# Attention probabilities kept whole in fp32, multiplied by the latent in two column groups

## The chip, the cores and the metric

The program runs on one core of one Trainium2 chip. The metric is the device time of one launch in microseconds, from the first to the last instruction of the core. Three runs of the kernel before gave 3666.07, 3667.09 and 3668.12 us, so the median is 3667.09 us. Times in the rows below are microseconds unless marked ns.

## The reference

One decoder layer over x of 4 x 512 x 1024 (fp32), in three parts, each followed by x + part and a layer norm:

- a gated state-space mixer (untouched by the change),
- cross attention against a context of 4 x 1601 x 1024, in which the change lies,
- a feed-forward network with int4-style weights (untouched).

The cross attention works through a latent of 64:

```python
C_q  = Q @ Wq_d                       # 512 x 128 per batch
C_kv = K @ Wkv_d                      # 1601 x 64 per batch: the latent
CqWqk = (C_q @ W_qk).reshape(b, n, H, LKV)              # 16 heads of 64
scores = einsum('bnhl,bkl->bhnk', CqWqk, C_kv) / sqrt(64)
attn = softmax(scores, axis=-1)
V_up = (C_kv @ Wv_u).reshape(b, nkv, H, HD)
out  = einsum('bhnk,bkhd->bnhd', attn, V_up)
```

The kernel uses that attn @ (C_kv @ Wv) = (attn @ C_kv) @ Wv: the probabilities are first multiplied by the latent (1601 x 64), the small result then by the head's 64 x 64 of Wv.

## The kernel before, in words

The three parts run one after the other, with a barrier of all engines between them. `attention` holds its order by hand: each engine has its own program, and semaphores tie them. There are 4 batches of 16 heads (g counts 64 heads), and a head has 4 units q of 128 queries. Units 0 and 1 are pair s=0, units 2 and 3 are pair s=1.

Ahead of the heads of a batch, the latent is computed on TensorE (L653, plain fp32), ScalarE rounds it to fp32r (`kh`), and VectorE subtracts to get the rest (`kl`, also fp32r). Both halves are turned by TensorE (L677, stationary 64 x 128, 64 columns streamed) and VectorE copies them to `cn`, 13 tiles of 128 keys x 128, where columns 0 to 63 are the high half and 64 to 127 the low half. The queries' projection is L667 (plain fp32, 512 columns) and, once per head, L589.

One unit goes through these steps:

- scores: 4 column chunks of the PSUM tile `sc`, each as two fp32r products with `kh` and `kl` (L696);
- `mx`, `nm` on VectorE (L860, L862, L866), then exp on ScalarE in two halves (L784), 1024 and 577 keys;
- the next unit's scores may overwrite a half of `sc` as soon as that half's exp is done;
- turns: 13 transposes of 128 x 128 (L618) into three PSUM tiles `tp`, in groups of 4, 4, 4 and 1, with group 3 of both units of a pair taken together. `TURNS` lists the 14 turns of a head. Each turn is emptied first by ScalarE, which writes the fp32r half `pth` (L742 and L739), then by VectorE, which subtracts to get `ptl` (L821 and L817);
- `weigh(g, s, part)`: `po` gathers cn.T @ pth and cn.T @ ptl for a pair, 26 fp32r products of 256 columns (two units of 128 queries), 13 in part 0 and 13 in part 1 (L629). The two 64-row halves of `po` hold the products with the latent's high and low half.

Once per head, ScalarE copies `po` to `ot` (L749), and `output` multiplies `ot` by Wv, stacked twice over 128 rows so that the two halves are added (4 products of 64 columns, L642). VectorE scales by the softmax sum (L836) and GpSimd adds to `y` (L921).

TensorE's order inside a unit is: scores of unit q, transposes of unit q-1, one weigh part, then a leftover: at q=0 the last turn of the head before, at q=1 the next head's projection, at q=2 turn 6, at q=3 the output of the head before. VectorE's order is: two maxima, `nm`, the three subtractions of unit q-1, then the same leftovers. ScalarE's is: three casts of unit q-1, the two exps of unit q, the leftovers.

The edits touch `tensor`, `scalar` and `vector` inside `attention`, the semaphores and the tiles above them.

Of the kernel before, what the change touches and what calls it, by code (L numbers as in the profile page):

```python
# [4 lines left out]
F32 = mybir.dt.float32  # L5
F32R = mybir.dt.float32r
I32 = mybir.dt.int32
ALU = mybir.AluOpType
# [3 lines left out]
P = 128  # L12
# [489 lines left out]
TURNS = [g for s in (0, 2) for g in (*((s + z, 1, k) for z in (0, 1) for k in range(3)), (s, 2, 3))]  # L502
NTURN = len(TURNS)
UNITS = QT
NHEAD = L * HEADS


def attention(nc, d, x1, x2):

    with ExitStack() as ctx:  # L510
# [9 lines left out]
        s_zero, s_y0 = sem("zero"), sem("y0")  # L520
        s_kv, s_kh, s_kl = sem("kv"), sem("kh"), sem("kl")
# [3 lines left out]
        s_tr, s_ph, s_pl, s_pv, s_ot = (sem(n) for n in ("tr", "ph", "pl", "pv", "ot"))  # L525
        s_sm, s_rd, s_op, s_yo, s_ya = (sem(n) for n in ("sm", "rd", "out_ps", "yo", "ya"))
        s_own, s_var, s_std, s_norm = sem("vector_own"), sem("var"), sem("std"), sem("norm")
# [54 lines left out]
        def tensor():  # L582
            T.wait_ge(small, 32)

            def project(g):
                T.wait_ge(s_wq, g + 1)
                if g % HEADS:
                    T.wait_ge(s_pl, (g - 1) * NTURN + 1)
                T.matmul(tp[0][:, :], wqs[:, g % 2, :, :].rearrange("p a e -> p (a e)"), cq[:, :],  # L589
                         start=True, stop=True).then_inc(s_q, 1)  # L590

            def turn(g, e):
                u, units, k, ng, s = turn_of(g, e)
                T.wait_ge(s_ex, (g * UNITS + u + units) * 2)
                if k in (1, 2):
                    if u or g % HEADS:
                        T.wait_ge(s_pl, g * NTURN + e - (3 if e in (1, 2, 8, 9) else 2))
                elif k == 3:
                    T.wait_ge(s_pl, g * NTURN + e - 2)
                elif u == 1 or u == 3:  # L600
                    if u == 1 and g % HEADS < HEADS - 1:
                        T.wait_ge(s_ql, g + 2)
                    elif u == 1:
                        T.wait_ge(s_pl, g * NTURN + 1)
                    elif u == 3 and g % HEADS:
                        T.wait_ge(s_yo, g)
                    else:
                        T.wait_ge(s_pl, g * NTURN + 8)
                elif u == 2:
                    T.wait_ge(s_pl, g * NTURN + 7)  # L610
                elif g % HEADS:
                    T.wait_ge(s_pl, g * NTURN)
                else:
                    T.wait_ge(s_ql, g + 1)
                n = 0
                for z in range(units):
                    for c in range(4 * k, 4 * k + ng):
                        ins = T.transpose(tp[k % 3][:, n * P:(n + 1) * P], pr[u + z][:, c * P:(c + 1) * P], ident[:, :])  # L618
                        n += 1
                ins.then_inc(s_tr, 1)  # L620

            def weigh(g, s, part):
                if part == 0:
                    if g:
                        T.wait_ge(s_ot, g)
                    T.wait_ge(s_pl, g * NTURN + 7 * (s + 1))
                for n in range(part * NKT, (part + 1) * NKT):
                    t, src = n // 2, (pth, ptl)[n % 2]
                    ins = T.matmul(po[:, s * 256:(s + 1) * 256], cn[:, t, :], src[s][:, t, :],  # L629
                                   start=(n == 0), stop=(n == 2 * NKT - 1))  # L630
                if part == 1:
                    ins.then_inc(s_pv, 1)

            def output(g):
                T.wait_ge(s_ot, g + 1)
                if g % HEADS < HEADS - 1:
                    T.wait_ge(s_pl, (g + 1) * NTURN + 8)
                else:
                    T.wait_ge(s_pl, (g + 1) * NTURN)
                h = g % HEADS  # L640
                for q in range(QT):
                    ins = T.matmul(tp[0][:, q * LAT:(q + 1) * LAT], ot[:, q * P:(q + 1) * P],  # L642
                                   wv[:, h * LAT:(h + 1) * LAT], start=True, stop=True)
                ins.then_inc(s_op, 1)

            for b in range(L):
# [22 lines left out]
                for k in range(len(GROUPS)):  # L669
                    T.wait_ge(s_kl, b * NKC + k + 1)  # L670
# [10 lines left out]
                T.wait_ge(s_cn, (b + 1) * 4)  # L681

                g0 = b * HEADS
# [41 lines left out]
        def scalar():  # L725
# [7 lines left out]
            def turn(g, e):  # L733
                u, units, k, ng, s = turn_of(g, e)
                S.wait_ge(s_tr, g * NTURN + e + 1)
                if e % 7 == 0 and g:
                    S.wait_ge(s_pv, 2 * (g - 1) + s + 1)
                if units == 2:
                    S.copy(pth[s][:, 4 * k, 0:2 * P], tp[k % 3][:, 0:2 * P]).then_inc(s_ph, 1)  # L739
                else:  # L740
                    lo = (u % 2) * P
                    S.copy(pth[s][:, 4 * k:4 * k + ng, lo:lo + P],  # L742
                           tp[k % 3][:, 0:ng * P].rearrange("p (t e) -> p t e", e=P)).then_inc(s_ph, 1)

            def output(g):
                S.wait_ge(s_pv, 2 * (g + 1))
                if g:
                    S.wait_ge(s_op, g)
                S.copy(ot[:, :], po[:, :]).then_inc(s_ot, 1)  # L749
# [52 lines left out]
        def vector():  # L802
            own = 0
            for t in (kh, kl, *pr):
                ins = V.memset(t[:, NKV:KPAD].bitcast(F32) if t.dtype == F32R else t[:, NKV:KPAD], 0.0)
# [7 lines left out]
            def turn(g, e):  # L813
                u, units, k, ng, s = turn_of(g, e)
                V.wait_ge(s_ph, g * NTURN + e + 1)
                if units == 2:
                    V.tensor_tensor(ptl[s][:, 4 * k, 0:2 * P], tp[k % 3][:, 0:2 * P], pth[s][:, 4 * k, 0:2 * P].bitcast(F32),  # L817
                                    ALU.subtract).then_inc(s_pl, 1)
                else:
                    lo = (u % 2) * P  # L820
# [18 lines left out]
            for b in range(L):  # L839
# [7 lines left out]
                for k in range(len(GROUPS)):  # L847
                    V.wait_ge(s_cnp, b * 4 + k + 1)
                    V.tensor_copy(cn[:, 4 * k:4 * k + GROUPS[k], :],
                                  tp[k % 2][:, 0:GROUPS[k] * P].rearrange("p (t e) -> p t e", e=P)).then_inc(s_cn, 1)  # L850
                g0 = b * HEADS
# [535 lines left out]
```

## Time and profile before

| | us |
|---|---|
| median of 3 runs | 3667.09 |
| the profiled execution | 3671.16 |
| its span | 3669.4 |
| PE busy in the span | 3116.9 (85%) |
| DVE busy | 2895.4 (79%) |
| ACT busy | 1899.6 (52%) |
| POOL busy | 1484.0 (40%) |

The profiled execution took 4.07 us more than the median, 1.8 us of which lie outside its span. PE is TensorE's matmul side and PEld its weight loads, which can lie under matmuls. A busy PE is not PE at its peak: a record's duration holds latency as well, so the pace of a stream is read from the starts of its records and not from their mean duration. A plain fp32 product leaves two load records and two matmul records (L667: 32 products, 64 records of each), an fp32r product and a transpose leave one of each. The mixer lies at 0 to 396 us, attention at 396 to 2001 us and the feed-forward network behind it.

### The profile page before, as it was taken

What the parts mean: (1) busy time and instruction counts of PE and PEld (TensorE: products, weight loads), DVE (VectorE), ACT (ScalarE), POOL (GpSimd) and SP (SyncE); (2) the same over time, 40 slices, a digit from 0 to 9 for tenths busy, and PEclk for the clock granted to TensorE, in tenths of its full rate; (3) what the DMA queues carried; (4) which work ended last, traced back from release to release, by engine and by line L of the source; (5) the groups of instructions that cost most, each with busy time, mean ns of one, the idle gap of its engine ahead of it and who ended that gap; (6) DMA issues with size and microseconds to landing.
All of it is one profiled execution on the core that took longest, in us unless ns stands there. A gap on an engine that the chain in (4) does not pass through costs nothing. (4 is left out here: it accounts for less than half of the span.)

```text
span 3669.4 us, 45273 instructions
## 1 busy us (share of the span) xinstructions
PE 3116.9 (85%) x16232; PEld 2464.0 (67%) x16232; DVE 2895.4 (79%) x3593; ACT 1899.6 (52%) x3089; POOL 1484.0 (40%) x672
## 2 busy tenths in 40 slices
PE   6455599998999899989997788888986799888986
PEld 3332388867888588858886566666664566666665
DVE  1657288866887588848886799999997799999997
ACT  2223177745776377727775444454453444444443
POOL 0242000000000000000000588888884588888884
PEclk8777799999999899989998899999998899999998
DMA  4003600011000300010001423333232433323332
GB/s 144 0 0 125 222 1 1 1 66 53 1 1 1 118 1 1 1 49 1 1 1 49 152 103 121 120 107 134 104 120 86 157 109 110 131 104 128 113 110 85
DMA packets 86158, 269.25 MB, mean 73 GB/s; under 512 B 12209, under 2 KB 13234, under 8 KB 85938
## 3 DMA queue, kind: packets, MB, share of 16 engines
q1 hardware_dynamic: 81090, 248.02, 19.2%
q10 hardware_dynamic: 4848, 18.35, 1.2%
q8 instruction: 132, 2.16, 0.2%
q14 instruction: 88, 0.72, 0.1%
HBM read 241.17 MB, written 25.17 MB: 73 GB/s over the span
## 5 line engine op out<-in xcount | busy, mean ns | idle before, releaser
L1292 POOL TENSOR_TENSOR c_sum_u<-c_sum_u,c_scaled 128x1024 f32<-128x1024 f32 x276 | 744.1, 2696 | 76.4 <-ACT c_scaled L1132 63.1
L1132 ACT ACTIVATE c_scaled<-c_ps,c_scol 128x1024 f32<-128x1024 f32 x448 | 498.1, 1118 | 501.2 <-PE c_ps L1081 305.3
L1201 DVE SCALAR_TENSOR_TENSOR c_acc<-c_ps,c_sd,c_acc 128x1024 f32<-128x1024 f32 x448 | 555.5, 1275 | 65.5 <-PE c_ps L1081 65.3
L742 ACT CAST b_pth<-b_tp 128x512 fp32r<-128x512 f32 x768 | 401.8, 596 | 376.4 <-PE b_tp L618 376.4
L921 POOL TENSOR_TENSOR b_y<-b_y,b_yo 128x256 f32<-128x256 f32 x64 | 47.3, 739 | 1347.2 <-DVE b_yo L836 1347.2
L821 DVE TENSOR_TENSOR b_ptl<-b_tp,b_pth 128x512 fp32r<-128x512 f32 x768 | 480.9, 682 | 7.7 <-ACT b_pth L742 7.6
L784 ACT ACTIVATE b_pr<-b_sc,b_nm 128x1024 f32<-128x1024 f32 (+1 forms) x512 | 474.9, 941 | 0.9 <-DVE b_nm L866 0.6
L618 PE MATMUL b_tp<-b_ident,b_pr 128*128 128x128 f32 x3328 | 441.4, 277 | 12.1 <-DVE b_ptl L821 8.1
L1292 POOL TENSOR_TENSOR c_sum_g<-c_sum_g,c_scaled 128x1024 f32<-128x1024 f32 x164 | 427.3, 2605 | 34.0 <-ACT c_scaled L1132 27.6
L696 PE MATMUL b_sc<-b_kh,b_qs 128*128 128x512 f32 (+1 forms) x1024 | 395.8, 387 | 44.0 <-ACT b_pr L784 31.2
L629 PE MATMUL b_po<-b_ptl,b_cn 128*128 128x256 f32 x1664 | 418.8, 289 | 0.0
L629 PE MATMUL b_po<-b_pth,b_cn 128*128 128x256 f32 x1664 | 418.7, 289 | 0.0
L1081 PE MATMUL c_ps<-c_xh,c_gw_int 128*128 128x512 f32 x896 | 305.3, 423 | 108.6 <-DVE c_sum_g L1214 94.7
L618 PEld LDWEIGHTS b_tp<-b_ident,b_pr 128*128 128x128 f32 x3328 | 363.3, 141 | 19.5 <-issue 11.6
L860 DVE TENSOR_REDUCE b_mx<-b_sc 128x1 f32<-128x1024 f32 x256 | 312.2, 1220 | 73.1 <-PE b_sc L696 71.2
L1081 PE MATMUL c_ps<-c_xh,c_uw_int 128*128 128x512 f32 x896 | 291.7, 407 | 73.2 <-DVE c_acc L1201 44.3
L696 PE MATMUL b_sc<-b_kl,b_qs 128*128 128x512 f32 (+1 forms) x1024 | 345.6, 370 | 0.0
L1081 PE MATMUL c_ps<-c_hh,c_dw_int 128*128 128x512 f32 x896 | 297.1, 414 | 31.3 <-POOL c_hl L1299 27.4
L629 PEld LDWEIGHTS b_po<-b_ptl,b_cn 128*128 128x128 f32 x1664 | 317.3, 191 | 0.0
L629 PEld LDWEIGHTS b_po<-b_pth,b_cn 128*128 128x128 f32 x1664 | 317.2, 191 | 0.0
L1214 DVE SCALAR_TENSOR_TENSOR c_sum_g<-c_ps,c_scol,c_sum_g 128x1024 f32<-128x1024 f32 x224 | 286.2, 1278 | 17.5 <-ACT c_sum_g L1125 6.8
L1081 PEld LDWEIGHTS c_ps<-c_xh,c_gw_int 128*128 128x128 f32 x896 | 159.0, 193 | 201.4 <-DVE c_sum_g L1214 118.6
(184 smaller groups left out, 5345.5 us busy)
## 6 DMA issues: line engine op xcount, KB each, us to landing
c_gw<-in_c_gw SPq DMA_DIRECT2D x56, 512.0 KB, 6.6
c_gz<-in_c_gz SPq DMA_DIRECT2D x56, 512.0 KB, 7.4
c_uw<-in_c_uw SPq DMA_DIRECT2D x56, 512.0 KB, 8.2
c_uz<-in_c_uz SPq DMA_DIRECT2D x56, 512.0 KB, 9.0
c_dw<-in_c_dw SPq DMA_DIRECT2D x56, 512.0 KB, 3.2
c_dz<-in_c_dz SPq DMA_DIRECT2D x56, 512.0 KB, 5.7
b_cx<-in_b_ctxT SPq DMA_DIRECT2D x12, 2048.0 KB, 11.6
a_xt<-in_a_xT SPq DMA_DIRECT2D x4, 2048.0 KB, 11.8
```

Of the source, the lines that this page charges most:

```text
L618: ins = T.transpose(tp[k % 3][:, n * P:(n + 1) * P], pr[u + z][:, c * P:(c + 1) * P], ident[:, :])
L629: ins = T.matmul(po[:, s * 256:(s + 1) * 256], cn[:, t, :], src[s][:, t, :], start=(n == 0), stop=(n == 2 * NKT - 1))
L696: ins = T.matmul(sc[:, n * 512:n * 512 + w], qs[g % 2][:, q * P:(q + 1) * P], k[:, n * 512:n * 512 + w], start=(z == 0), stop=(z == 1))
L742: S.copy(pth[s][:, 4 * k:4 * k + ng, lo:lo + P], tp[k % 3][:, 0:ng * P].rearrange("p (t e) -> p t e", e=P)).then_inc(s_ph, 1)
L784: S.activation(pr[q][:, lo:hi], sc[:, lo:hi], ACT.Exp, bias=nm[:, q % 2:q % 2 + 1], scale=0.125, accum_out=den[:, g % 2, q, half:half + 1] ...
L821: V.tensor_tensor(ptl[s][:, 4 * k:4 * k + ng, lo:lo + P], tp[k % 3][:, 0:ng * P].rearrange("p (t e) -> p t e", e=P), pth[s][:, 4 * k:4 * k ...
L860: V.tensor_reduce(mx[:, 0:1], sc[:, 0:1024], AX, ALU.max).then_inc(s_ma, 1)
L1081: ins = T.matmul(pair[PLACE[x]][:, b * 512:(b + 1) * 512], w[n][t % 2][:, k * P:(k + 1) * P], v[:, b * 512:(b + 1) * 512], start=(z == 0), ...
L1132: S.activation(scaled[q % 2][:, :], ps[:, :], ACT.Identity, scale=column).then_inc(s_c, 1)
L1201: V.scalar_tensor_tensor(out=acc[:, k, :], in0=ps[:, :], scalar=sd[:, k, j - 1:j], in1=acc[:, k, :], op0=ALU.mult, op1=ALU.add).then_inc(s ...
L1214: V.scalar_tensor_tensor(out=total, in0=ps[:, :], scalar=column, in1=total, op0=ALU.mult, op1=ALU.add).then_inc(s_a[n], 1)
L1292: G.tensor_tensor(total, total, scaled[POOLED.index(x) % 2][:, :], ALU.add).then_inc(s_a[n], 1)
```

## The change

The turned probabilities are no longer split. Each turn is emptied once, as fp32, into `pt`: groups 0 and 3 by ScalarE (`BY_ACT`, 6 turns of a head), groups 1 and 2 by VectorE (`BY_DVE`, 8 turns). The latent is kept whole too: ScalarE copies the 64 rows of each chunk to `kf` ahead of `kh`, and `cn` has 64 columns per tile of keys. `weigh` gives each unit of a pair its own 64 columns of the array and its own 64 partitions of `po`: for each of the 13 tiles of keys two plain fp32 products of 128 columns, with the stationary `cn[:, t, :]` of 64 columns. `output` now contracts over 64 rows, units 0 and 2 first, then, after a wait for those, units 1 and 3. Where TensorE waited for `ptl`, it now waits for the one copy (`copied`). Scores, exp, projections and the other two parts of the layer are the same.

```diff
+BY_ACT = [e for e in range(NTURN) if TURNS[e][2] in (0, 3)]
+BY_DVE = [e for e in range(NTURN) if TURNS[e][2] in (1, 2)]
...
-        cn = sb("b_cn", [P, NKT, P], F32R)
+        cn = sb("b_cn", [P, NKT, LAT])
-        pth = [sb(f"b_pth{j}", [P, NKT, 2 * P], F32R) for j in range(2)]
-        ptl = [sb(f"b_ptl{j}", [P, NKT, 2 * P], F32R) for j in range(2)]
-        ot = sb("b_ot", [P, NB])
+        pt = [sb(f"b_pt{j}", [P, NKT, 2 * P]) for j in range(2)]
+        kf = sb("b_kf", [LAT, KPAD])
+        ot = sb("b_ot", [P, 2 * P])
...
+        def copied(eng, g, e):
+            if e in BY_ACT:
+                eng.wait_ge(s_pa, g * len(BY_ACT) + BY_ACT.index(e) + 1)
+            else:
+                eng.wait_ge(s_pd, g * len(BY_DVE) + BY_DVE.index(e) + 1)
...
 def weigh(g, s, part):
-                    T.wait_ge(s_pl, g * NTURN + 7 * (s + 1))
+                    copied(T, g, 7 * s + 6)
+                    copied(T, g, 7 * s + 5)
                 for n in range(part * NKT, (part + 1) * NKT):
-                    t, src = n // 2, (pth, ptl)[n % 2]
-                    ins = T.matmul(po[:, s * 256:(s + 1) * 256], cn[:, t, :], src[s][:, t, :],
-                                   start=(n == 0), stop=(n == 2 * NKT - 1))
+                    t, z = n // 2, n % 2
+                    ins = T.matmul(po[z * LAT:(z + 1) * LAT, s * P:(s + 1) * P], cn[:, t, :], pt[s][:, t, z * P:(z + 1) * P],
+                                   start=(t == 0), stop=(t == NKT - 1))
...
 def output(g):
-                for q in range(QT):
-                    ins = T.matmul(tp[0][:, q * LAT:(q + 1) * LAT], ot[:, q * P:(q + 1) * P],
-                                   wv[:, h * LAT:(h + 1) * LAT], start=True, stop=True)
-                ins.then_inc(s_op, 1)
+                for z in range(2):
+                    if z:
+                        T.wait_ge(s_oe, g + 1)
+                    for s in range(2):
+                        q = 2 * s + z
+                        ins = T.matmul(tp[0][:, q * LAT:(q + 1) * LAT], ot[z * LAT:(z + 1) * LAT, s * P:(s + 1) * P],
+                                       wv[z * LAT:(z + 1) * LAT, h * LAT:(h + 1) * LAT], start=True, stop=True)
+                    ins.then_inc(s_op if z else s_oe, 1)
...
 latent, per tile of keys (tensor)
-                        for z, src in enumerate((kh, kl)):
-                            ins = T.transpose(tp[k % 2][:, (t - 4 * k) * P + z * LAT:(t - 4 * k) * P + (z + 1) * LAT],
-                                              src[0:LAT, t * P:(t + 1) * P].bitcast(F32), ident[0:LAT, 0:LAT])
+                        ins = T.transpose(tp[k % 2][:, (t - 4 * k) * LAT:(t - 4 * k + 1) * LAT],
+                                          kf[:, t * P:(t + 1) * P], ident[0:LAT, 0:LAT])
...
 scalar
-                    S.copy(pth[s][:, 4 * k:4 * k + ng, lo:lo + P],
-                           tp[k % 3][:, 0:ng * P].rearrange("p (t e) -> p t e", e=P)).then_inc(s_ph, 1)
+                    S.copy(pt[s][:, 4 * k:4 * k + ng, lo:lo + P],
+                           tp[k % 3][:, 0:ng * P].rearrange("p (t e) -> p t e", e=P)).then_inc(s_pa, 1)
+                    S.copy(kf[:, n * 512:n * 512 + KCHUNK[n]], sc[0:LAT, n * 512:n * 512 + KCHUNK[n]]).then_inc(s_kf, 1)
...
 vector
-                    V.tensor_tensor(ptl[s][:, 4 * k:4 * k + ng, lo:lo + P],
-                                    tp[k % 3][:, 0:ng * P].rearrange("p (t e) -> p t e", e=P),
-                                    pth[s][:, 4 * k:4 * k + ng, lo:lo + P].bitcast(F32), ALU.subtract).then_inc(s_pl, 1)
+                V.tensor_copy(pt[s][:, 4 * k:4 * k + ng, lo:lo + P],
+                              tp[k % 3][:, 0:ng * P].rearrange("p (t e) -> p t e", e=P)).then_inc(s_pd, 1)
```

## Rows read from the trace of the kernel before

**Rows 1.** Busy time by stretch: mixer, heads of batch 0, feed-forward network
```profile
core 0: us, PE busy (x) PEld busy (x) DVE busy (x) ACT busy (x) POOL busy (x), PEclk, DMA share, GB/s
0.00:396.00 396.00, 207.06 (x705) 120.40 (x705) 194.31 (x345) 111.32 (x253) 89.47 (x36) 0.75 0.24 82
...
440.00:785.00 345.00, 330.93 (x2290) 294.47 (x2290) 280.45 (x475) 244.25 (x511) 14.44 (x29) 0.99 0.00 1
...
2001.00:3669.00 1668.00, 1403.11 (x5632) 1059.79 (x5632) 1510.63 (x1211) 781.33 (x740) 1317.33 (x504) 0.94 0.33 118
```
**Rows 2.** Waits, 396 to 2001 us: total us, times, longest
```profile
PE b_sc L696 <- ACT b_pr L784: 31.2, 75, 3.8
```
**Rows 3.** Timeline, unit q=2 of a head: start, us, engine, line
```profile
1406.41 0.50 PE L696 MATMUL b_sc<-b_kh,b_qs 128*128 128x512 f32 x1 [0.17 <-ACT b_pr L784]
...
1407.72 1.22 DVE L860 TENSOR_REDUCE b_mx<-b_sc 128x1 f32<-128x1024 f32 x1
...
1408.74 1.57 ACT L742 CAST b_pth<-b_tp 128x512 fp32r<-128x512 f32 x3 [0.91 <-PE b_tp L618]
1408.85 0.75 DVE L862 TENSOR_REDUCE b_mx<-b_sc 128x1 f32<-128x577 f32 x1
1409.71 0.21 DVE L866 TENSOR_SCALAR b_nm<-b_mx 128x1 f32<-128x1 f32 x1
...
1410.18 1.14 ACT L784 ACTIVATE b_pr<-b_sc,b_nm 128x1024 f32<-128x1024 f32 x1
...
1411.78 0.47 PE L696 MATMUL b_sc<-b_kh,b_qs 128*128 128x512 f32 x1
```
**Rows 4.** Groups of instructions by form: count | busy us, mean ns | idle
```profile
L821 DVE TENSOR_TENSOR b_ptl<-b_tp,b_pth 128x512 fp32r<-128x512 f32 x768 | 480.9, 682 | 7.7 <-ACT b_pth L742 7.6
L742 ACT CAST b_pth<-b_tp 128x512 fp32r<-128x512 f32 x768 | 401.8, 596 | 376.4 <-PE b_tp L618 376.4
L846 DVE COPY b_xT<-b_tp 128x512 f32<-128x512 f32 x16 | 11.1, 692 | 10.6 <-PE b_tp L661 10.6
```
**Rows 5.** Timeline, TensorE: last transposes, a weigh part, the output, the next scores
```profile
506.31 0.71 PE L618 MATMUL b_tp<-b_ident,b_pr 128*128 128x128 f32 x5
506.78 0.37 PE L629 MATMUL b_po<-b_pth,b_cn 128*128 128x256 f32 x1
506.98 0.28 PE L629 MATMUL b_po<-b_ptl,b_cn 128*128 128x256 f32 x1
...
508.30 0.28 PE L629 MATMUL b_po<-b_pth,b_cn 128*128 128x256 f32 x1
508.42 1.00 PE L642 MATMUL b_tp<-b_wv,b_ot 128*128 128x64 f32 x8
509.23 0.47 PE L696 MATMUL b_sc<-b_kh,b_qs 128*128 128x512 f32 x1
```
**Rows 6.** Timeline, TensorE: plain fp32 of 512 columns, then the latent's turns
```profile
429.31 7.11 PE L667 MATMUL b_po<-b_xT,b_wqd 128*128 128x512 f32 x16 [0.88 <-DVE b_xT L846]
436.34 0.27 PE L677 MATMUL b_tp<-b_ident,b_kh 64*128 64x64 f32 x1
436.46 0.22 PE L677 MATMUL b_tp<-b_ident,b_kl 64*128 64x64 f32 x1
...
436.95 0.22 PE L677 MATMUL b_tp<-b_ident,b_kl 64*128 64x64 f32 x1
```
**Rows 7.** Timeline: products of 4 columns, whose loads set the pace
```profile
113.69 1.40 PE L155 MATMUL a_ps<-a_fcd,a_xst 128*128 128x4 f32 x12
```
**Rows 8.** Timeline: VectorE behind an output, and a load under a matmul
```profile
508.18 0.28 PE L629 MATMUL b_po<-b_ptl,b_cn 128*128 128x256 f32 x1
508.18 0.19 PEld L629 LDWEIGHTS b_po<-b_pth,b_cn 128*128 128x128 f32 x1
...
509.46 0.42 DVE L836 TENSOR_TENSOR b_yo<-b_tp,b_rd 128x256 f32<-128x256 f32 x1 [0.29 <-PE b_tp L642]
509.96 0.74 POOL L921 TENSOR_TENSOR b_y<-b_y,b_yo 128x256 f32<-128x256 f32 x1 [20.04 <-DVE b_yo L836]
```

More of the change, by code:

```diff
@@ L520, in attention @@
         s_zero, s_y0 = sem("zero"), sem("y0")
-        s_kv, s_kh, s_kl = sem("kv"), sem("kh"), sem("kl")
+        s_kv, s_kh, s_kf, s_kl = sem("kv"), sem("kh"), sem("kf"), sem("kl")
         s_xt, s_xa, s_xd, s_cqp, s_cq, s_cnp, s_cn = (sem(n) for n in ("xt", "xt_act", "xt_dve", "cq_ps", "cq", "cn_ps", "cn"))
@@ L524, in attention @@
         s_sa, s_sb, s_ma, s_mb, s_nm, s_ex = (sem(n) for n in ("sa", "sb", "max_a", "max_b", "nm", "ex"))
-        s_tr, s_ph, s_pl, s_pv, s_ot = (sem(n) for n in ("tr", "ph", "pl", "pv", "ot"))
-        s_sm, s_rd, s_op, s_yo, s_ya = (sem(n) for n in ("sm", "rd", "out_ps", "yo", "ya"))
+        s_tr, s_pa, s_pd, s_pv, s_ot = (sem(n) for n in ("tr", "p_act", "p_dve", "pv", "ot"))
+        s_sm, s_rd, s_oe, s_op, s_yo, s_ya = (sem(n) for n in ("sm", "rd", "out_even", "out_ps", "yo", "ya"))
         s_own, s_var, s_std, s_norm = sem("vector_own"), sem("var"), sem("std"), sem("norm")
@@ L587, in project @@
                 if g % HEADS:
-                    T.wait_ge(s_pl, (g - 1) * NTURN + 1)
+                    copied(T, g - 1, 0)
                 T.matmul(tp[0][:, :], wqs[:, g % 2, :, :].rearrange("p a e -> p (a e)"), cq[:, :],
@@ L595, in turn @@
                 if k in (1, 2):
-                    if u or g % HEADS:
-                        T.wait_ge(s_pl, g * NTURN + e - (3 if e in (1, 2, 8, 9) else 2))
+                    if u:
+                        copied(T, g, e - (4 if u == 2 else 3))
+                    elif g % HEADS:
+                        copied(T, g - 1, e + 10)
                 elif k == 3:
-                    T.wait_ge(s_pl, g * NTURN + e - 2)
+                    copied(T, g, e - 3)
                 elif u == 1 or u == 3:
@@ L603, in turn @@
                     elif u == 1:
-                        T.wait_ge(s_pl, g * NTURN + 1)
+                        copied(T, g, 0)
                     elif u == 3 and g % HEADS:
@@ L607, in turn @@
                     else:
-                        T.wait_ge(s_pl, g * NTURN + 8)
+                        copied(T, g, 7)
                 elif u == 2:
-                    T.wait_ge(s_pl, g * NTURN + 7)
+                    copied(T, g, 6)
                 elif g % HEADS:
-                    T.wait_ge(s_pl, g * NTURN)
+                    copied(T, g - 1, 13)
                 else:
@@ L636, in output @@
                 if g % HEADS < HEADS - 1:
[L637 removed]
+                    copied(T, g + 1, 7)
                 else:
[L639 removed]
+                    copied(T, g, 13)
                 h = g % HEADS
[L641 to L644 removed]
+                for z in range(2):
[6 more added lines that the diff above has]
+                    ins.then_inc(s_op if z else s_oe, 1)
             for b in range(L):
@@ L669, in tensor @@
                 for k in range(len(GROUPS)):
-                    T.wait_ge(s_kl, b * NKC + k + 1)
+                    T.wait_ge(s_kf, b * NKC + k + 1)
                     if k == 0:
@@ L681, in tensor @@
                 T.wait_ge(s_cn, (b + 1) * 4)
+                T.wait_ge(s_kl, (b + 1) * NKC)
                 g0 = b * HEADS
@@ L734, in turn @@
                 u, units, k, ng, s = turn_of(g, e)
+                if e not in BY_ACT:
+                    return
                 S.wait_ge(s_tr, g * NTURN + e + 1)
@@ L738, in turn @@
                 if units == 2:
-                    S.copy(pth[s][:, 4 * k, 0:2 * P], tp[k % 3][:, 0:2 * P]).then_inc(s_ph, 1)
+                    S.copy(pt[s][:, 4 * k, 0:2 * P], tp[k % 3][:, 0:2 * P]).then_inc(s_pa, 1)
                 else:
                     lo = (u % 2) * P
-                    S.copy(pth[s][:, 4 * k:4 * k + ng, lo:lo + P],
-                           tp[k % 3][:, 0:ng * P].rearrange("p (t e) -> p t e", e=P)).then_inc(s_ph, 1)
+                    S.copy(pt[s][:, 4 * k:4 * k + ng, lo:lo + P],
+                           tp[k % 3][:, 0:ng * P].rearrange("p (t e) -> p t e", e=P)).then_inc(s_pa, 1)
             def output(g):
@@ L748, in output @@
                     S.wait_ge(s_op, g)
-                S.copy(ot[:, :], po[:, :]).then_inc(s_ot, 1)
+                S.copy(ot[:, :], po[:, 0:2 * P]).then_inc(s_ot, 1)
             for b in range(L):
@@ L803, in vector @@
             own = 0
-            for t in (kh, kl, *pr):
+            for t in (kh, kl, kf, *pr):
                 ins = V.memset(t[:, NKV:KPAD].bitcast(F32) if t.dtype == F32R else t[:, NKV:KPAD], 0.0)
@@ L814, in turn @@
                 u, units, k, ng, s = turn_of(g, e)
[L815 to L820, printed above, removed]
-                    V.tensor_tensor(ptl[s][:, 4 * k:4 * k + ng, lo:lo + P],
-                                    tp[k % 3][:, 0:ng * P].rearrange("p (t e) -> p t e", e=P),
-                                    pth[s][:, 4 * k:4 * k + ng, lo:lo + P].bitcast(F32), ALU.subtract).then_inc(s_pl, 1)
+                if e not in BY_DVE:
+                    return
+                V.wait_ge(s_tr, g * NTURN + e + 1)
+                if e % 7 == 1 and g:
+                    V.wait_ge(s_pv, 2 * (g - 1) + s + 1)
+                lo = (u % 2) * P
+                V.tensor_copy(pt[s][:, 4 * k:4 * k + ng, lo:lo + P],
+                              tp[k % 3][:, 0:ng * P].rearrange("p (t e) -> p t e", e=P)).then_inc(s_pd, 1)
             def sums(g):
@@ L849, in vector @@
                     V.tensor_copy(cn[:, 4 * k:4 * k + GROUPS[k], :],
-                                  tp[k % 2][:, 0:GROUPS[k] * P].rearrange("p (t e) -> p t e", e=P)).then_inc(s_cn, 1)
+                                  tp[k % 2][:, 0:GROUPS[k] * LAT].rearrange("p (t e) -> p t e", e=LAT)).then_inc(s_cn, 1)
                 g0 = b * HEADS
```

## The prediction

> **What bounds the kernel now.** I read the stretches first: the mixer and the feed-forward network keep their work, so their 396 and 1668 us stay, and the change is worth what it is worth among the heads. There TensorE is busy 330.93 of 345 us, with the granted clock at 0.99, the level of 2.4 GHz [rows 1]. The waits say the same: over all of attention TensorE's scores wait 31.2 us for the exp that frees `sc`, and no other engine holds it up for more [rows 2]. A head takes 0.74 + 20.04 = 20.78 us by GpSimd's add, which comes once per head [rows 8]. That is 5.2 us per unit.
>
> A second loop is nearly as long, though. Read unit q=2 in order of time [rows 3]: the scores start at 1406.41, the first maximum at 1407.72, the second at 1408.85, `nm` ends at 1409.92, but the exp starts at 1410.18, because ScalarE has been in its three casts since 1408.74. The exp ends at 1411.32 and the next scores start at 1411.78, when TensorE is through with the output. So this loop could turn in about 4.9 us against TensorE's 5.2. Two conclusions: added TensorE time goes into the end almost in full, and saved TensorE time pays until the unit nears 4.9 us. What VectorE and ScalarE save pays almost nothing by itself.
>
> **The weigh parts (256 of them, 64 heads by 4).** One takes 508.42 - 506.78 = 1.64 us: 13 records at (508.30 - 506.98)/11 = 0.120 us each are 1.56, and 0.08 lies at the entry [rows 5]. After the change a part has 13 plain fp32 products, so 26 records of 128 columns. The streaming rate of plain fp32 is in the 16 records of 512 columns: (436.34 - 429.31)/16 = 0.439 us, or 0.110 us for 128 columns [rows 6]. The load need not add to it: a load starts with the matmul ahead of it, at 508.18 both [rows 8], and loads of 128 columns, bare of streaming, follow each other every 1.40/12 = 0.117 us at most [rows 7]; these have 64 columns.
>
> Everything hangs on whether the products of the two units, in two column groups, run beside each other. No row shows a product in a column group, so the price is bounded from both sides. One after the other: 26 x 0.110 = 2.86 us. Side by side, with unit 1's first record under unit 0's second and so on: half, 0.055 us per record, 1.43 us. Nothing below that, since each group alone must stream 13 x 0.110. A floor near it is in the trace: load and matmul pairs of the latent's turns follow each other every (436.95 - 436.46)/8 = 0.061 us [rows 6], so the queue can hand out pairs at about the rate wanted. I take side by side, at 0.058 us between these two: 26 x 0.058 = 1.51 against 1.56, or -0.05 x 256 = -13 us. I take it because the two groups share neither stationary, nor moving data, nor output partitions, and only order in one queue ties them.
>
> The Trainium skill, "TensorE: Matmul & The Clock Gate", Part 3, says that matmuls on different tiles of the array run concurrently and reports 2.38 times for three column tiles of 32. No run here shows it so far; by it alone a part would cost some 1.4 to 1.8 us.
>
> **Changing between whole-array and column-group work.** Each part is now preceded and followed by products of the whole array, 8 changes per head, 512 in all. The nearest row: entering the 64-row turns, the first record takes 0.12 us instead of 0.061, so 0.06 [rows 6], where the entry of a weigh part costs 0.08 already [rows 5]. That makes the extra 0. The other end is a whole latency of a record: 0.22 long at a pace of 0.061, so 0.16 us [rows 6], 82 us in all. I take 0.04, nearer to the row: +20 us.
>
> **The output (64 times).** Eight records take 509.23 - 508.42 = 0.81 us, 0.101 each, and the last one ends 1.00 - 7 x 0.101 = 0.29 after it starts [rows 5]. Now four records, then a wait for their end, then four. VectorE starts 0.04 us after that last end (509.42 to 509.46) [rows 8]; with the same delay the second four start at 3 x 0.101 + 0.29 + 0.04 = 0.63, pay an entry of 0.08, and end at 0.63 + 0.08 + 0.40 = 1.11. That is +0.30, or +20 us; bounds +13 (no entry) to +40 (two changes of the array at 0.16 on top). Behind the waiting product in TensorE's queue are the next head's scores of unit 0, and behind these the maxima, so this is on the path.
>
> **Relief.** VectorE has 8 copies instead of 12 + 2 subtractions in a head, at 0.69 (the copy of a PSUM tile) against 0.68 us; ScalarE loses 8 casts of 0.6 us, 4.8 us per head [rows 4]. TensorE is never fed by them for long, so it counts where TensorE stands: the 0.26 us by which casts hold the exp in unit q=2 [rows 3] comes off waits of 31.2 us in all [rows 2], into which part of the added time falls too. Bounds -25 and 0; I take -8.
>
> **Once per batch.** 52 of the 104 turns of the latent go, at 0.061 [rows 6]: -3 us. The `kf` copies lie under the next chunk's products except the last, short one: +1. Behind the last unit the subtraction that followed the cast goes: -2. Together -4 us.
>
> **Sum.** -13 + 20 + 20 - 8 - 4 = +15 us on the profiled execution's 3671.2, so 3686; this execution is 4 us over the median, so 3682. A change under 0.2% (7.3 us) can't be told from none.
>
> **Rivals.**
> - *One after the other.* The second unit's products don't start before the first's have streamed. Then a part takes 26 x 0.110 + 0.08 = 2.94 us, +1.30 x 256 = +333; with +20 for the output, -4, and about -10 for waits that this fills, +340: 4007 us. For it: no row shows two products streaming at once, and the records of one engine run in order. At the pace of the bare loads, 0.117 [rows 7], it would be 4054.
> - *Faster: pairs at the full rate.* Its place is the weigh part, its price the pace of a record. At 0.055 the parts give -0.13 x 256 = -33; with no cost for changes, +20 for the output, -20 for relief and -4: -37, so 3630 us. With the terms at my values for output, changes, relief and batches (+28), it turns into a gain under (1.56 - 28/256)/26 = 0.0558 us per record; without the cost of changes, already under 0.0596. Against it: the only pace shown for such short pairs is 0.061.
> - *The changes cost a full emptying.* 0.16 for each of 512 and of 128 more around the outputs: +102 in place of +20; with -13, +20 and -4 that is +105: 3772 us. What speaks for it is that a record's 0.16 of latency exists; against it, that entering the 64-row turns cost 0.06.
>
> The Trainium skill states this last one as a rule: "TensorEngine Tiling (Array Packing)", Key Properties, says that changing the tiling mode drains TensorE. The 0.06 of the row doesn't bear out a full emptying, and by the rule the sum would be the rival's.
>
> - *Half beside each other*, because loads or the two records of a product hold each other up: between, about 3850 us.
>
> **How the numbers follow.** Side by side as forecast 0.33 (own range 3645 to 3740), one after the other 0.30, full rate 0.20, full emptying 0.12, half 0.05. The likeliest gives 3682. The range takes in most of the full-rate case and the one-after-the-other case up to 4020: 3635 to 4020. Faster by over 0.2%: the full-rate case and a low end of the forecast's, 0.26. Within 0.2%: 0.09. Slower: 0.65, of which nearly half is the serial case.
>
> **What would show it.** In the timeline of TensorE, 26 records of a part in about 1.5 us, with starts two to a step of 0.11; a serial case shows 2.9 us, a head of 26 us, and no waits for the exp. Parts that enter or leave with gaps over 0.1 us show the emptying. The output should span 1.1 us. VectorE's busy time should fall by about 3.4 us per head and ScalarE's by 4.8 without TensorE's waits vanishing. The stretches of mixer and feed-forward network should be unmoved; if they move, or the granted clock among the heads leaves 0.98, the prediction is wrong for a reason that it doesn't hold.

## The result and the profile after

The changed kernel takes 3695.86 us (median of 4 runs, 3692.24 to 3700.31) against 3667.61 us for the kernel before beside it (4 runs): ratio 1.0078, 95% interval 1.0061 to 1.0096. It is 28 us slower, where +15 was forecast (3682 us). The profiled execution took 3693.81 us with a span of 3692.0.

The page first, then the stretches [rows 1]: the heads of batch 0 still fill 440 to 785 us, and the other stretch is within the feed-forward network.

```profile
span 3692.0 us, 51078 instructions
PE 3162.8 (86%) x19508; PEld 2445.4 (66%) x19508; DVE 2698.0 (73%) x3210; ACT 1661.3 (45%) x2593; POOL 1485.6 (40%) x672
...
L640 PE MATMUL b_po<-b_pt,b_cn 128*64 128x128 f32 x6656 | 443.5, 276 | 0.0
```

```profile
440.00:785.00 345.00, 340.71 (x3065) 289.24 (x3066) 228.47 (x375) 180.99 (x381) 14.10 (x28) 0.99 0.01 1
2001.00:3669.00 1668.00, 1401.40 (x5766) 1059.71 (x5764) 1515.57 (x1194) 777.68 (x741) 1320.58 (x506) 0.94 0.32 115
```

VectorE's and ScalarE's busy time have fallen by 52 and 63 us in the first stretch, TensorE's has risen by 10, and the granted clock is 0.99 as before. TensorE is now busy 340.71 of 345 us, so it still bounds the heads. Now the timeline of TensorE around one part and the output, which answers to [rows 5]:

```profile
1403.73 1.53 PE L628 MATMUL b_tp<-b_ident,b_pr 128*128 128x128 f32 x12
1405.19 1.74 PE L640 MATMUL b_po<-b_pt,b_cn 128*64 128x128 f32 x26
1406.86 1.37 PE L657 MATMUL b_tp<-b_wv,b_ot 64*128 64x64 f32 x8
1408.16 0.50 PE L711 MATMUL b_sc<-b_kh,b_qs 128*128 128x512 f32 x1
```

Three things are to be seen. First, the 26 records of the part start 0.059 us apart on average, (1.74 - 0.272)/25, so the two units do run side by side. The average hides how. Here are the first two and the last two records of this part, each pair from a window of its own:

```profile
1405.19 0.33 PE L640 MATMUL b_po<-b_pt,b_cn 128*64 128x128 f32 x2
1406.55 0.38 PE L640 MATMUL b_po<-b_pt,b_cn 128*64 128x128 f32 x2
```

A record is 0.32 us long at the entry and 0.27 at the end of a part, so the first two start 0.007 us apart and the last two 0.109. The trace's start times say the same of all 244 parts whose records stand in it whole: 12 pairs, one of each column group, 0.160 us from the first pair to the second and 0.109 from then on, and at the end two single records. A part has 13 products, 7 of one unit and 6 of the other. The last product has no partner, so a part takes 14 steps of 0.109 us and not 13.

Second, the 12 transposes, which took 1.28 us to the next start before, take 1405.19 - 1403.73 = 1.46. Third, the output takes 1.30 us instead of 0.81.

The waits, 396 to 2030 us, over which the four batches now stretch. The first row is of the kernel before (396 to 2001 us), the other two of the changed one:

```profile
PEld b_sc L696 <- ACT b_pr L784: 89.7, 192, 4.0
```
```profile
PEld b_sc L711 <- ACT b_pr L802: 27.8, 17, 4.0
PE b_sc L711 <- ACT b_pr L802: 23.1, 11, 3.9
```

The matmul row fell by 8 us only [rows 2], but the row of the loads fell by 62 and from 192 times to 17, where attention has 256 units. The start times show what is meant. They need one correction of the rows ahead of the prediction: the unit that [rows 3] shows, and that the prediction reads, is q=3 and not q=2, for the output stands behind it. In the kernel before, the two transposes ahead of its scores took 0.55 us to the next start, in the changed one they take 0.34, and 0.20 ahead of the scores of q=1:

```profile
1405.86 0.38 PE L618 MATMUL b_tp<-b_ident,b_pr 128*128 128x128 f32 x2
...
1406.41 0.50 PE L696 MATMUL b_sc<-b_kh,b_qs 128*128 128x512 f32 x1 [0.17 <-ACT b_pr L784]
```
```profile
1401.75 0.44 PE L628 MATMUL b_tp<-b_ident,b_pr 128*128 128x128 f32 x2
1402.09 0.50 PE L711 MATMUL b_sc<-b_kh,b_qs 128*128 128x512 f32 x1
...
1412.91 0.44 PE L628 MATMUL b_tp<-b_ident,b_pr 128*128 128x128 f32 x2
1413.11 0.48 PE L711 MATMUL b_sc<-b_kh,b_qs 128*128 128x512 f32 x1
```

By start-to-start times over all heads, what moved is this. The two middle columns are medians, worked out from the two traces; the last one is the difference of the sums, since some kinds of stretch come in two lengths.

| stretch of TensorE, to the next start | before | after | times | us |
|---|---|---|---|---|
| 12 transposes, then a part | 1.284 | 1.459 | 244 | +43 |
| a weigh part, then another stretch | 1.638 | 1.673 | 236 | +8 |
| output | 0.812 | 1.298 | 56 | +27 |
| 2 transposes, then scores | 0.495 | 0.195 | 120 | -31 |
| the next head's projection, then scores | 0.588 | 0.562 | 64 | -5 |
| a weigh part, then scores at once | 2.223 | 1.794 | 8 | -3 |
| scores of a unit | 1.632 | 1.633 | 248 | +3 |

That is +42; the stretches of the heads, from first to last `nm` of a batch, grew by 41 us in all. From the last latent product to the first `nm` each batch is 1.1 to 2.3 us shorter, -6 us in all. The spans differ by only 22.6 us. The rest, -13 us, lies in the mixer, the feed-forward network and the starts of batches. The edit doesn't touch the mixer, and yet it ends (by the start of the first latent product) at 396.0 us before and 390.5 after; over all kernels here its end lies between 389.6 and 398.2 us. So a difference of a few us between two kernels is to be looked for in the heads before it is believed.

### The profile page after: what moved, and what is told of

The parts are those of the page before. It is cut to its first block and busy times, and to the rows that moved or that the text cites. A ratio compares the mean times of both kernels' runs of the same rounds, so it can differ in the third digit from the quotient of the medians.

```text
span 3692.0 us, 51078 instructions
## 1 busy us (share of the span) xinstructions
PE 3162.8 (86%) x19508; PEld 2445.4 (66%) x19508; DVE 2698.0 (73%) x3210; ACT 1661.3 (45%) x2593; POOL 1485.6 (40%) x672
## 5 line engine op out<-in xcount | busy, mean ns | idle before, releaser
L640 PE MATMUL b_po<-b_pt,b_cn 128*64 128x128 f32 x6656 | 443.5, 276 | 0.0
L640 PEld LDWEIGHTS b_po<-b_pt,b_cn 128*64 128x64 f32 x6656 | 383.7, 137 | 41.6 <-issue 41.3
L759 ACT COPY b_pt<-b_tp 128x512 f32<-128x512 f32 x256 | 150.1, 586 | 447.4 <-PE b_tp L628 447.4
L839 DVE COPY b_pt<-b_tp 128x512 f32<-128x512 f32 x512 | 327.4, 681 | 8.0 <-PE b_tp L628 7.4
L1098 PE MATMUL c_ps<-c_xl,c_gw_int 128*128 128x512 f32 x896 | 291.4, 408 | 0.0
L1098 PE MATMUL c_ps<-c_hl,c_dw_int 128*128 128x512 f32 x896 | 285.2, 400 | 0.0
```

Source lines behind the costliest of these rows:

```text
L640: ins = T.matmul(po[z * LAT:(z + 1) * LAT, s * P:(s + 1) * P], cn[:, t, :], pt[s][:, t, z * P:(z + 1) * P], start=(t == 0), stop=(t == NKT ...
L759: S.copy(pt[s][:, 4 * k:4 * k + ng, lo:lo + P], tp[k % 3][:, 0:ng * P].rearrange("p (t e) -> p t e", e=P)).then_inc(s_pa, 1)
L839: V.tensor_copy(pt[s][:, 4 * k:4 * k + ng, lo:lo + P], tp[k % 3][:, 0:ng * P].rearrange("p (t e) -> p t e", e=P)).then_inc(s_pd, 1)
L1098: ins = T.matmul(pair[PLACE[x]][:, b * 512:(b + 1) * 512], w[n][t % 2][:, k * P:(k + 1) * P], v[:, b * 512:(b + 1) * 512], start=(z == 0), ...
```

## Experiments

The kernel before was run beside each of them and took 3666.6 to 3668.3 us (medians), so their times can be set against each other. Ratios are to the kernel before; differences to the changed kernel are between medians.

### Is it the alternation that makes them run side by side?

```diff
-                    t, z = n // 2, n % 2
+                    t, z = n % NKT, n // NKT
```

> The changed kernel, but part 0 of a weigh holds all 13 products of one unit (one column group) and part 1 all 13 of the other, instead of alternating. Same products, same number of records and changes. Theory (the two column groups run side by side, two records per 0.11 us, which the alternation makes possible): without alternation a part takes 26 x 0.110 + 0.14 = 3.0 us instead of 1.67, so +1.33 x 256 = +341 us, about 4037 us, and a pace of 0.110 us in the part. Rival (a plain fp32 record with 64 stationary columns simply takes 0.059 us, nothing overlaps): the time stays at 3696 us and the pace at 0.059.

One run: 4020.3 us, +324 on the changed kernel. The timeline of TensorE:

```profile
1455.59 1.50 PE L628 MATMUL b_tp<-b_ident,b_pr 128*128 128x128 f32 x12
1457.02 3.05 PE L640 MATMUL b_po<-b_pt,b_cn 128*64 128x128 f32 x26
1460.00 0.44 PE L628 MATMUL b_tp<-b_ident,b_pr 128*128 128x128 f32 x2
```

The same 26 records now follow each other every 0.109 us behind the first, which takes 0.160. The rival is out: a record of 64 stationary columns costs its full streaming, and two of them fit into that time when they belong to different column groups. The gap ahead of the part stays (the 12 transposes take 1.46 us in the steady heads).

### The same product without column groups

```diff
-                for n in range(part * NKT, (part + 1) * NKT):
-                    t, z = n // 2, n % 2
-                    ins = T.matmul(po[z * LAT:(z + 1) * LAT, s * P:(s + 1) * P], cn[:, t, :], pt[s][:, t, z * P:(z + 1) * P],
+                for t in ((range(7), range(7, NKT))[part]):
+                    ins = T.matmul(po[:, s * 256:(s + 1) * 256], cn[:, t, :], pt[s][:, t, :],
```

> The changed kernel without column groups: the latent's tiles are 128 columns wide with zeros in columns 64 to 127, a product streams both units (256 columns) in plain fp32 over the whole array, 14 or 12 records per part, and the output is the one of the kernel before (4 products over 128 rows, no wait). VectorE and ScalarE keep the changed kernel's single copies. Theory: 13 x 0.220 = 2.86 us per part on average, entry 0.08 without the 0.175 of delay before the part, so 2.94 against 1.67 + 0.175: +1.09 x 256 = +280 us, output 0.49 x 64 = 31 us less: about 3945 us; the gap between the last transposes and the part is under 0.03 us. Rival (the 0.175 us belongs to plain fp32 after transposes, not to column groups): the gap stays and the time is about 3990 us.

One run: 3919.4 us, +224 on the changed kernel; 3945 was expected.

```profile
1455.35 1.50 PE L628 MATMUL b_tp<-b_ident,b_pr 128*128 128x128 f32 x12
1456.69 2.76 PE L639 MATMUL b_po<-b_pt,b_cn 128*128 128x256 f32 x12
1459.28 0.38 PE L628 MATMUL b_tp<-b_ident,b_pr 128*128 128x128 f32 x2
```

By the medians of all heads, the 12 transposes take 1.365 us to the next start: 0.081 more than ahead of the fp32r part of before, and 0.094 less than ahead of column groups. The 0.081 is no loss. From the start of the last transpose it takes 0.109 us to the part's first record, and that one takes 0.218 where the others take 0.216. In the kernel before, the first record starts after 0.028 us and then takes 0.202 where the others take 0.120. Together that is 0.230, which is again one step of a transpose and one of the part. So the 0.08 by which the prediction priced the entry of a part before [rows 5] was an early start paid back, and the whole array is entered at no price in either type.

The column groups do pay, at four places, here against the 0.109 us that a step takes otherwise:

| step | column groups | whole array, plain fp32 |
|---|---|---|
| last transpose to first record | 0.202 | 0.109 |
| first pair to second, first record to second | 0.160 | 0.218, its pace 0.216 |
| last record to the next stretch | 0.203 | 0.216 |
| first to second transpose behind the part | 0.165 | 0.109 |

The surplus is 0.093 + 0.051 + 0.094 + 0.056 = 0.29 us for one entry and one exit.

### A second entry and exit per part

The weigh part is cut in two, with the third group of transposes between, once in the changed kernel and once in the kernel before:

```diff
+                        if what:
+                            weigh(*what, piece=1)
+                        if of:
+                            turn(of[0], TURNS.index((of[1], 1, 2)))
+                        if what:
+                            weigh(*what, piece=2)
```

> The changed kernel with each weigh part cut in two (12 and 14 records) and the third group of transposes between, so that each part is entered and left twice. Theory (entering and leaving column-group work costs 0.175 us before the part and 0.14 behind it, through the change of the array's shape): one more of each per part, +0.32 x 244 = +78 us, about 3774 us. Rival (the delay is a wait for data or for the queue at this place and happens once): under +25 us, as for the kernel before when it is cut in the same way.

> The kernel before with its weigh parts cut in the same way (6 and 7 records, the third group of transposes between): the control, whole array throughout. Theory: one more entry of 0.08 us per part, 244 x 0.08 = +20 us less what falls into waits for the exp: 3667 to 3690 us. Rival (any interleaving costs as much as in the changed kernel): +78 us, about 3745 us.

The changed kernel so cut takes 3767.16 us, ratio 1.0268 (1.0252 to 1.0283) to the kernel before: +71 us on the uncut one, or 0.29 us for each of 244 cuts. The start times agree: by medians the four stretches of a cut unit take 1.022 + 0.807 + 0.586 + 1.018 = 3.43 us against 1.459 + 1.673 = 3.13. The piece of 6 products has 12 records, all in pairs. The timeline of one unit:

```profile
1401.91 1.09 PE L628 MATMUL b_tp<-b_ident,b_pr 128*128 128x128 f32 x8
1402.94 0.88 PE L641 MATMUL b_po<-b_pt,b_cn 128*64 128x128 f32 x12
1403.74 0.66 PE L628 MATMUL b_tp<-b_ident,b_pr 128*128 128x128 f32 x4
1404.33 1.09 PE L641 MATMUL b_po<-b_pt,b_cn 128*64 128x128 f32 x14
```

The control missed both theories: the kernel before, cut, takes 3786.72 us, ratio 1.0323 (1.0306 to 1.0341), +119 us. But the gaps around its parts are small (by medians 8 transposes take 0.847 us to the next start, 6 records 0.796). ScalarE's timeline shows where the time is:

```profile
1401.67 1.08 ACT L744 CAST b_pth<-b_tp 128x512 fp32r<-128x512 f32 x2 [1.39 <-PE b_tp L618]
1403.26 0.59 ACT L744 CAST b_pth<-b_tp 128x512 fp32r<-128x512 f32 x1 [0.51 <-PE b_tp L618]
1403.74 1.12 ACT L786 ACTIVATE b_pr<-b_sc,b_nm 128x1024 f32<-128x1024 f32 x1
```

The third cast waits for the later transposes, and the exp stands behind it, though `nm` ended at 1403.13. The exp starts 0.61 us after that. TensorE's waits for the exp rise to this (396 to 2030 us):

```profile
PEld b_sc L697 <- ACT b_pr L786: 180.9, 183, 4.0
PE b_sc L697 <- ACT b_pr L786: 116.9, 184, 3.9
```

So this was no clean control: it measured ScalarE's order. The control had to be made again without casts ahead of the exp, below.

### What the relief of VectorE and ScalarE is worth

First VectorE alone, on the kernel before (the subtractions go, `weigh` reads the high half twice):

```diff
-                    t, src = n // 2, (pth, ptl)[n % 2]
+                    t, src = n // 2, (pth, pth)[n % 2]
```

> The kernel before without its 14 subtractions per head: the weigh products read the high half twice, so TensorE's and ScalarE's work is the same and VectorE's falls by 9 us per head. It leaves out the low halves of the probabilities. Theory (it is ScalarE's three casts ahead of the exp that make TensorE wait, not VectorE): the two waits of 0.28 us per head stay, -0 to -8 us, 3659 to 3667 us. Rival (VectorE's subtractions hold up the maxima): the waits go, -31 us, about 3636 us.

3657.90 us, ratio 0.9974 (0.9965 to 0.9983): -9 us, of which the two transposes ahead of the scores show none (0.497 us); it is in the next head's projection, 0.491 instead of 0.588 us to the scores behind it, and at the batch ends.

Then both engines, with TensorE's old work among the heads:

```diff
+                    ins = T.matmul(po[:, s * 256:(s + 1) * 256], cn[:, n // 2, :], pt[s][:, n // 2, :],
+                                   start=(n == 0), stop=(n == 2 * NKT - 1))
```

> The kernel before's TensorE work among the heads (26 fp32r products of 256 columns over the whole array per pair, its output) with the changed kernel's single copies, 6 turns by ScalarE and 8 by VectorE. It leaves out the low halves of probabilities and latent. Theory (one cast ahead of the exp instead of three lets the exp loop turn faster): the waits of 0.28 us twice per head go, -31 us, and -5 us for the latent's turns: about 3631 us. By the prediction's own term for relief, -8 and -5: 3654 us.

3640.64 us, ratio 0.9925 (0.9907 to 0.9942): -26 us, between the two numbers but nearer the first. By the traces the heads are 22 us shorter and the ways from the last latent product to the first `nm` 6. This kernel and the one before it leave out the low halves, so they price the relief and are no versions to use. Here the exp starts 0.12 us behind `nm`, as ScalarE has only one cast ahead of it:

```profile
1403.23 0.59 ACT L754 CAST b_pt<-b_tp 128x512 fp32r<-128x512 f32 x1 [2.13 <-PE b_tp L628]
...
1404.56 0.21 DVE L879 TENSOR_SCALAR b_nm<-b_mx 128x1 f32<-128x1 f32 x1
...
1404.89 1.11 ACT L797 ACTIVATE b_pr<-b_sc,b_nm 128x1024 f32<-128x1024 f32 x1 [1.07 <-DVE b_nm L879]
```

The other way round, all copies of the changed kernel on ScalarE:

```diff
-BY_ACT = [e for e in range(NTURN) if TURNS[e][2] in (0, 3)]
-BY_DVE = [e for e in range(NTURN) if TURNS[e][2] in (1, 2)]
+BY_ACT = [e for e in range(NTURN)]
+BY_DVE = []
```

> The changed kernel with all 14 copies of a head on ScalarE, so that three copies stand ahead of the exp again, as the three casts did in the kernel before; VectorE makes none. TensorE's work is the same. Theory (the relief is worth something only where TensorE's unit is shorter than the exp loop, and the slower weigh parts and output have made it longer): the exp starts 0.16 us later in its unit, which is covered but for some 0.1 us in units 0 and 2: +5 to +12 us, about 3704 us. Rival (the relief is worth its 26 us whatever TensorE does): 3722 us.

3714.48 us, ratio 1.0129 (1.0112 to 1.0146): +19 us on the changed kernel, above the 5 to 12 and below the 26. But the traces place it otherwise. Of the 19.4 us between the two profiled executions the heads hold 10 (1384.8 against 1374.6 us, first to last `nm`), and 8 lie in the mixer, which the edit doesn't touch. So in the heads the relief of ScalarE is worth about 10 us here, within the theory's range (VectorE, which makes no copies in this kernel, is relieved further, so 10 may be a little low). The waits are back (396 to 2030 us), 75 times instead of 17:

```profile
PEld b_sc L711 <- ACT b_pr L802: 46.8, 75, 4.3
```

And the cut again, on the relieved whole-array kernel:

> The relieved whole-array kernel (fp32r products of 256 columns, single copies by both engines; it leaves out the low halves) with its weigh parts cut in two around the third group of transposes: the control for the cut without three casts ahead of the exp. Its uncut version took 3640.6 us. Theory (whole-array parts are entered at 0.08 us and left at no cost, column-group parts at 0.17 and 0.14): +0.08 x 244 = +20 us, about 3661 us, less what falls into waits. Rival (what the cut costs is the later third group, whatever the array's shape, as the +119 us of the kernel before suggests): over 3710 us.

3635.87 us, against 3640.64 uncut: the cut costs nothing with the whole array, and the 20 us of the theory are not there. By medians the four stretches of a cut unit take 0.848 + 0.796 + 0.355 + 0.917 = 2.92 us against 1.285 + 1.639 = 2.92 uncut. The parts take 0.07 more and the transposes 0.08 less: the early start and its payment again. The waits for the exp didn't change (2 transposes, then scores: 0.45 us in the mean, 0.44 uncut). The 71 us of the cut column-group kernel are therefore the price of entering and leaving column-group work, 0.29 us for each pair.

### The output

```diff
-                    if z:
-                        T.wait_ge(s_oe, g + 1)
-                        ins = T.matmul(tp[0][:, q * LAT:(q + 1) * LAT], ot[z * LAT:(z + 1) * LAT, s * P:(s + 1) * P],
+                        ins = T.matmul(tp[z][:, s * LAT:(s + 1) * LAT], ot[z * LAT:(z + 1) * LAT, s * P:(s + 1) * P],
```

> The changed kernel with the output of units 1 and 3 in another PSUM tile (tp1), so that TensorE does not wait between the two row groups; VectorE scales in two instructions. Theory (0.30 us of the output is the wait): -0.30 x 64 = -19 us, about 3677 us, and the output spans 1.0 us. Rival (the whole 0.49 us over the old output is the change of the array's shape): no change, 3696 us.

3653.32 us, ratio 0.9959 (0.9942 to 0.9975): -43 us on the changed kernel, more than twice what was expected.

```profile
1399.05 0.67 PE L656 MATMUL b_tp<-b_wv,b_ot 64*128 64x64 f32 x8
1399.65 0.50 PE L710 MATMUL b_sc<-b_kh,b_qs 128*128 128x512 f32 x1
```

The output takes 0.60 us instead of 1.30. Its eight records start (0.67 - 0.272)/7 = 0.057 us apart on average, half of the 0.101 of before: the two row groups run side by side too, once they write into different PSUM tiles and no wait divides them. They start in pairs as well, the first two 0.013 us apart (a record is 0.32 us long here):

```profile
1399.05 0.33 PE L656 MATMUL b_tp<-b_wv,b_ot 64*128 64x64 f32 x2
```

In the queue these products don't alternate: both of one row group stand ahead of both of the other. So the two groups need not be neighbours to overlap. Two products apart is near enough here, 13 apart was not for the column groups.

The Trainium skill, "TensorEngine Tiling (Array Packing)", Gotcha 1, says that row tiles go to different PSUM banks and may not access one at the same time. That is the reason for the wait in the changed kernel. No run shows what happens in one PSUM tile without it.

```diff
-                for z in range(2):
-                    if z:
-                        T.wait_ge(s_oe, g + 1)
-                    for s in range(2):
+                for s in range(2):
+                    ins = T.matmul(tp[0][:, s * P:(s + 1) * P], ot[:, s * P:(s + 1) * P],
+                                   wv[:, h, :], start=True, stop=True)
```

> The changed kernel with its output over the whole array: Wv lies as a block diagonal (two 64 x 64 blocks per head, zeros beside them), so one product of 128 rows and 128 columns gives both units of a pair, 4 records per head instead of 8, no 64-row groups and no wait in the middle. Theory (the output's 1.30 us are two shape changes and the wait): 4 x 0.110 + 0.09 = 0.53 us, -0.77 x 64 = -49 us, of which some 5 may come back as waits for the exp: about 3651 us, faster than the kernel before. Rival (the exp loop takes over as soon as TensorE gets shorter): the output gets shorter, waits for the exp take its place and the time stays above 3680 us.

3644.19 us (5 runs), ratio 0.9933 (0.9916 to 0.9950): 22 us faster than the kernel before and 52 us than the changed one. This is the best of the versions that compute the whole result.

```profile
1415.75 1.74 PE L640 MATMUL b_po<-b_pt,b_cn 128*64 128x128 f32 x26
1417.42 0.71 PE L653 MATMUL b_tp<-b_wv,b_ot 128*128 128x128 f32 x4
1417.89 0.48 PE L707 MATMUL b_sc<-b_kh,b_qs 128*128 128x512 f32 x1
```

The output takes 0.47 us, and no wait took its place. Against the changed kernel the heads are 48 us shorter (1327.0 against 1374.6 us), so nearly all of the 52 us is the output. Against the kernel before they are only 6 us shorter; of the 26 us between these two profiled executions 7 lie in the ways from the last latent product to the first `nm`, and the rest around the batches and in the other two parts.

## Why the prediction was right, and where it was not

The direction holds: the groups run side by side, TensorE bounds the heads, and what it gains in pace is lost at the edges. The total, +15 against +28 measured, is nearer than its terms. That is luck: changes and output were 66 us too small together, and what the waits gave back was 42 us too small the other way.

- **Pace.** -13 us was forecast, and 14 steps of 0.109 us against 1.56 give -8. The 0.058 us per record is near the average of 0.059, but not for the reason given. Pairs go at the full rate, 0.109 us for two, and the product without a partner adds a step. The prediction's floor, "each group alone must stream 13 x 0.110", has this wrong: within a part one unit has 7 products, so 14 records. Its rival of the full rate was right about the pairs and wrong about the part. An estimate from these numbers: parts of 12 and 14 products instead of 13 and 13 would leave no product alone and save a step per part, 0.109 x 256 = 28 us. No run tries it. The doubling without alternation confirms the cause. The Trainium skill, "TensorE: Matmul & The Clock Gate", Part 3, says that matmuls on different tiles of the array run concurrently. The trace agrees: 0.007 us between the two starts of a pair, 0.109 without alternation.
- **The changes.** 0.04 us each, +20 us, was too small. The four steps above give 0.29 us per entry and exit and the cut kernel the same, so 0.15 per change and 75 us for 512. The rival "full emptying" had 0.16 and was right in this term; its 3772 us came out too high by what the waits gave back and by its extra 128 changes. Taking the row that needed the least was the mistake: that row entered 64-row turns, not column groups behind other work. And the 0.08 for the entry before, which the forecast set off against it, was no price at all. The Trainium skill, "TensorEngine Tiling (Array Packing)", Key Properties, states that changing the tiling mode drains TensorE. The size agrees; but the next record starts 0.203 us after the last one of a part, which is 0.27 long by its modelled end, so whether the array is quite empty isn't shown.
- **The output.** +0.49 us against +0.30, 31 us against 20. I charged it one wait. It also has a change of its own at its end (0.202 us from the last start to the scores) and a slow first step in each half (0.160 us, the others 0.112), and the 0.60 us without the wait shows that the wait forbade the overlap.
- **The waits.** -8 us, bounds -25 and 0. The table has -36 for the stretches ahead of scores, and since these also pay the last of the four steps (0.056 us ahead of 120 scores, 0.104 in 64 projections), the waits gave back about 50. I had bounded them by the 31.2 us of the matmuls' row [rows 2]. A record's modelled end lies over a part of the wait behind it, so that row holds only the rest. The loads' row, 89.7 us, is too high, since loads can be early. The starts are the measure: 0.53 us in the mean for the 2 transposes ahead of scores, where a kernel that waits for nothing takes 0.14 (the one without column groups). What gave the time back is relief only in part. Taking ScalarE's part of the relief away brings 10 us of waits back into the heads; VectorE's alone was worth 7 in the heads of the kernel before. The rest I put down to TensorE's added time falling into the waits: in the kernel without alternation, which has the same copies and more time on TensorE, the 2 transposes take 0.193 us everywhere, where the changed kernel has 0.34 in every second case. So the conclusion that "added TensorE time goes into the end almost in full" failed: of some 90 us about half did. How the 50 us divide between relief and added time isn't measured further.
- **Relief by itself.** The other conclusion, that what VectorE and ScalarE save "pays almost nothing by itself", failed too: on the kernel before it pays 26 us, 22 of them in the heads.
- **Per batch.** -4 us was forecast, -6 measured in the stretches ahead of the heads.
- **Sum.** My four terms among the heads were -13 + 20 + 20 - 8 = +19. Measured, they are -8 + 75 + 31 - 50 = +48 over all 256 parts and 64 outputs (some 3 us of the output are changes counted twice), or +42 where the steady heads alone are counted as in the table. With -6 for the batches the changed kernel should be some 36 us slower; the median says 28. The missing 8 us, in parts that the change doesn't touch, stay open.

Of the signs named ahead, the steps of 0.11 us with two starts each came true. The output spans 1.30 and not 1.1 us. VectorE's and ScalarE's busy time fell by 3.1 and 3.7 us per head, where 3.4 and 4.8 were named, and TensorE's waits for the exp did nearly vanish in the loads' row. Of the rivals, the serial case is what the kernel without alternation does, at 4020 us against the 4007 that the prediction gave it.

## What to carry to other kernels

Column groups double the rate of half-width products only if products of different groups stand close together in the queue, and in equal numbers, for one without a partner takes a full step. Every stretch of them pays about 0.3 us at its two edges, so long stretches pay and short ones don't: here 1.67 us of work stood against that. A late or early first start is not yet a price; add up the steps on both sides of the edge. An idle time in front of a matmul is to be read from the starts, not from the matmuls' own row. Where half-height products come in pairs, a block-diagonal operand over the whole array, or a second PSUM tile, is better than a wait between them. And when two profiled executions are compared, look first at the parts that no edit touched.

## What was not expected of the hardware

- Column-group records start in pairs 0.007 us apart, one pair every 0.109 us, and the last product of an odd number takes its two steps alone.
- Two row groups that write different PSUM tiles also run side by side: 8 records at 0.057 us against 0.101, though the products of one group stand together in the queue.
- Going from transposes into a part over the whole array and back costs nothing, in plain fp32 or in fp32r; going into two column groups and back costs 0.29 us.
- Cutting a part in two cost 119 us in the kernel before and nothing in the relieved one, where ScalarE has one cast ahead of the exp instead of three.
